# TensorE's order inside an expert step exchanged: the preceding expert's down products ahead of the next expert's up products

## The reference

```python
def step(state, xb_t):
    state = jnp.tanh(state @ A.T + xb_t)
    return (state, state)
out = jnp.einsum('bsn,dn->bsd', states, C) + D * x
y = out + x                                   # then layer norm, gamma, beta
x = _layernorm(x + y_normed)
...
scores = jax.nn.sigmoid(x @ router_weight.T)  # best group of four, best two of it
comb = (one_hot(topk_idx, E) * topk_w[..., None]).sum(1)
g = einsum('th,ehi->tei', x, w_gate); u = einsum('th,ehi->tei', x, w_up)
y = einsum('tei,eih->teh', silu(g) * u, w_down)
routed = einsum('teh,te->th', y, comb)
shared = silu(x @ sw_gate) * (x @ sw_up) @ sw_down
x = _layernorm(x + routed + shared)
```

## Time and profile before

| | us |
|---|---|
| median of 3 runs | 409.91 |
| lowest and highest | 409.0 and 410.25 |
| the profiled execution, whole | 411.52 |
| its span | 409.6 |
| scan, up to the first group | about 84 |
| one steady group (204 to 244) | 40.0 |
| TensorE busy in it | 38.75 |
| VectorE busy in it | 35.66 |

### The profile page before, as it was taken

The page is one execution under the profiler, slowest core; times in us unless marked ns, Lnnn a source line. Parts: engine busy times, 40 slices in busy tenths (PEclk is TensorE's granted clock), DMA queues, the critical chain, the costliest instruction groups (busy, mean ns, idle before and its releaser), DMA issues.

```text
span 409.6 us, 7468 instructions
## 1 busy us (share of the span) xinstructions
PE 377.2 (92%) x2563; PEld 248.1 (61%) x2563; DVE 324.3 (79%) x744; ACT 137.0 (33%) x276; POOL 160.1 (39%) x158
## 2 busy tenths in 40 slices
PE   6889996889899989998999899989998999999991
PEld 5889885445556555655665566556655666555560
DVE  2348998559786999699979997998799789974564
ACT  2455232132324232423242324243324333333330
POOL 1859018027433453344234513441354125423332
PEclk9999999689999999999999999999999999999997
DMA  7990000035005601560145016401840173009211
GB/s 204 305 317 4 0 2 0 2 94 115 2 0 104 106 2 51 100 109 1 53 113 96 1 53 129 78 0 53 133 71 0 53 150 57 36 20 165 40 53 51
DMA packets 15901, 29.95 MB, mean 73 GB/s; under 512 B 1720, under 2 KB 4288, under 8 KB 15872
## 3 DMA queue, kind: packets, MB, share of 16 engines
q1 hardware_dynamic: 15872, 29.58, 31.3%
HBM read 25.24 MB, written 4.33 MB: 72 GB/s over the span
## 4 chain that ended last, share of the span: by engine, by line
issue 28%; DVE 27%; PE 16%; POOL 14%; DMA 6%; SPq 5%; ACT 2%; POOLq 1%; DVEq 0%; ACTq 0%
PE bank L400 10%; POOL h L1008 10%; DVE st L722 4%; DVE wg L764 3%; PE bank L477 3%; POOL rstd L989 3%; DVE xT L879 3%; SPq L216 3%; DMA wu<-comb_dram 3%; DVE wu L755 2%; DMA xres<-in_L_attn_x_dram 2%; DVE xT L883 2%; DVE wu L747 1%; DVE wg L696 1%; ACT h L613 1%
## 5 line engine op out<-in xcount | busy, mean ns | idle before, releaser
L1008 POOL TENSOR_TENSOR h<-xT,h 128x512 f16<-128x512 f32 x72 | 86.1, 1195 | 192.7 <-ACT h L613 192.7
L400 PE MATMUL bank<-x2T,wg 128*128 128x512 f16 x432 | 107.4, 386 | 0.0
L477 PE MATMUL bank<-wd,h 128*128 128x256 f16 x864 | 106.1, 273 | 1.1 <-DVE wd L891 0.6
L400 PE MATMUL bank<-x2T,wu 128*128 128x512 f16 x432 | 106.5, 383 | 0.0
L477 PEld LDWEIGHTS bank<-wd,h 128*128 128x128 f16 x864 | 84.1, 98 | 25.6 <-issue 2.3
L613 ACT ACTIVATE h<-xT 128x512 f16<-128x512 f32 x72 | 45.4, 630 | 135.9 <-DVE xT L883 131.7
L400 PEld LDWEIGHTS bank<-x2T,wu 128*128 128x128 f16 x432 | 42.8, 99 | 52.7 <-issue 3.0
L879 DVE SCALAR_TENSOR_TENSOR xT<-bank,u_un,xT 128x512 f32<-128x512 f32 x64 | 47.5, 743 | 22.5 <-ACT xT L602 21.6
L400 PEld LDWEIGHTS bank<-x2T,wg 128*128 128x128 f16 x432 | 42.0, 99 | 37.1 <-issue 2.1
L602 ACT ACTIVATE xT<-bank,g_un 128x512 f32<-128x512 f32 x72 | 49.2, 683 | 35.8 <-PE bank L400 34.2
L313 PE MATMUL bank<-xT,BT 128*128 128x128 f32 x256 | 40.0, 279 | 0.0
(11 more groups left out here) (124 smaller groups left out, 370.0 us busy)
## 6 DMA issues: line engine op xcount, KB each, us to landing
comb_own<-comb_dram SPq DMA_DIRECT2D x32, 256.0 KB, 9.0
wu<-comb_dram SPq DMA_DIRECT2D x16, 256.0 KB, 4.1
wd<-comb_dram SPq DMA_DIRECT2D x16, 256.0 KB, 6.3
xres<-in_L_attn_x_dram SPq DMA_DIRECT2D x7, 512.0 KB, 6.6
out_dram<-xskip SPq DMA_DIRECT2D x7, 512.0 KB, 2.7
wd<-in_L_ffn_w_down_dram SPq DMA_DIRECT2D x1, 1024.0 KB, 6.9
xres<-in_L_attn_x_dram SPq DMA_DIRECT2D x2, 256.0 KB, 3.1
out_dram<-xskip SPq DMA_DIRECT2D x2, 256.0 KB, 2.0
```

What stands on the lines that cost most here:

```text
L400: last = pe.matmul(ps[:, :], w[:, pw, e, m // 3, :], x2T[:, par, px, m // 3, :], start=(m == 0), stop=(m == NUP // 2 - 1))
L477: return pe.matmul(ps_y[t // 2][:, (t % 2) * DM:(t % 2 + 1) * DM], h16[:, e % 3, ph, t * P:(t + 1) * P], wd16[:, pw, e, :], start=start, s ...
L1008: nc.gpsimd.tensor_tensor(h16[:, e % 3, 1, :], h[:, b, :], h16[:, e % 3, 0, :], ALU.subtract).then_inc(h_low, 1)
```

## The change

In `group` of TensorE the call of `down` for the preceding expert is moved ahead of the call of `up` for the next expert (and ahead of `turn_comb` in step 8). Nothing else is edited.

```diff
                 for e in range(E1):
                     b = (par + e) % 2
+                    if e:
+                        down(g, e - 1)
+                    elif not first:
+                        down(g - 1, E1 - 1)
                     if e < E1 - 1:
                         if e or not first:
                             up(g, e + 1, par, 1 - b)
                     elif not final:
                         up(g + 1, 0, 1 - par, 1 - b)
                         turn_comb(g + 1)
-                    if e:
-                        down(g, e - 1)
-                    elif not first:
-                        down(g - 1, E1 - 1)
                     if not final:
                         piece(e, g + 1, 1 - par, main)
```

## The result

| | before | after |
|---|---|---|
| median (lowest to highest), us | 410.08 (409.0 to 411.89) | 480.31 (478.84 to 481.75) |
| ratio | | 1.171, 95% interval 1.168 to 1.174 |
| span of the profiled execution | 409.6 | 476.8 |
| mean granted clock | 0.981 | 0.945 |

The account below looks back on a forecast made before the run. TensorE (92% busy) hardly waited before; in the new order VectorE's work sets each group's floor. Order 50 us plus clock 15 makes 65 on the 409.9 us median: 475 us, range 455 to 490 for 8 in 10.

Parts of the forecast that it names:

- the likeliest case: Whole kernel: new order and lower clock together give 465 to 485 us; chance 0.55.
- The floor by VectorE and the period: Steady group: VectorE's unshrinkable work gives a 44.9 us floor; with three late up products the period is 46.6 against 40.0.
- The order's total: Whole kernel without clock: six periods at 6.6 us, first group 5.8, last 4.7, sum 50.1 us.
- The wait ahead of D(0): TensorE ahead of expert 0's down products: waits 3.1 us for VectorE's closing sum, which comes after expert 1.
- The wait ahead of D(8): TensorE ahead of expert 8's down products: waits 2.6 to 3.0 us because VectorE's choice of experts can't shrink.
- The first group: First group: 1.9 us waiting for expert 0's low half, up products 1.31 later, expert 8's wait 2.6; together 5.8 us.
- The clock: TensorE at group boundaries: 9 of 14 waits drop the clock, 1.7 us each, 15 us; bounds 0 and 28.
- The clock stays up: Rival, whole kernel: clock stays at its upper level, 410 + 50 = 460 us; chance 0.20.
- The clock low at nearly every wait and slow to return: Rival, group boundaries: clock adds 28 us or more to the order's 50, giving 490 us; chance 0.12.
- Most of the wait absorbed: Rival: VectorE's idle time takes up late up products, only the 3.1 us closing-sum waits remain, some 432 us; chance 0.09.
- faster: Rival: earlier down products free halves and banks, transpose waits go, saving 10 us, 400 us; chance 0.02.
- no change: Rival: TensorE takes ready up products ahead of waiting down products, so the time stays 410 us; chance 0.02.

Follow-up runs that it names:

- the filled kernel: Changed kernel plus throwaway matmuls on TensorE, 10 ahead of expert 8's down products and 13 ahead of expert 0's, in every group but the first: 461.53 us, ratio 1.128.
- step 1 back: Changed kernel with step 1 alone in the old order, expert 2's up products ahead of expert 0's down products: 441.12 us, ratio 1.080.
- closing sum first: Changed kernel with VectorE's closing sum taken ahead of expert 1's gated product instead of behind its weighting: 444.54 us, ratio 1.086.
- the exchange there: Changed kernel with ScalarE, in step 8, making expert 8's high half ahead of the copy of the turned weights of choice: 478.03 us, ratio 1.167.
- the shorter choice: Changed kernel without VectorE's three tie-deciding operations: 477.57 us, ratio 1.168; with ScalarE's high half also ahead of its copy: 458.81 us, ratio 1.120.
- the last kernel: Kernel before, old order, with the transposes of steps 4 and 5 moved behind the next step's up products: 408.15 us, ratio 0.997.

## Why the prediction was right

The forecast was 475 us, the result 480.3, inside the range and inside the likeliest case's own.

- **The floor by VectorE and the period.** Summed 46.6 us, measured 46.94 with the clock held up. Right in its parts too. In the filled kernel it is 12.6 us from D(8) to the product of expert 2 (summed 12.5), 30.5 from there to product 8 (summed as 28.96 of work and 1.7 for three late U), and 3.79 from product 8 to the next D(8) (3.43). The three late U were summed as 0.5, 0.8 and 0.4 us and stand in the changed kernel at 0.43, 0.72 and 0.44. The last part is the one that was too short, by ScalarE's queue. The order's total was put at 50.1, it is 51.7.
- **The wait ahead of D(0)**, 3.1 us from U(1), SiLU, product, weighting and sum: measured 3.05 to 3.15, at the last boundary 3.7. Shown by two kernels that took it away (step 1 back, closing sum first).
- **The wait ahead of D(8)**, 2.6 to 3.0 from the choice of the experts: measured 2.4 to 2.8. The size was right, the reason was only one half. I followed VectorE's chain and left out ScalarE's queue; the exchange there and the shorter choice together show that both chains ended within 0.4 us of each other.
- **The first group**, 1.9 us ahead of D(0): measured 1.02 (D(0) at 85.80).
- **The clock**, 9 low stretches of 1.7 us, 15 us in all: eleven of 1.71, 18.8. The price was right, the count low by two. The clock makes 3.8 us of the 5.3 by which the forecast was short, the order 1.6. That the count came so near is in part luck: it was taken from three gaps, and waits of the same length cost none of seven and four of seven in two of the kernels above.
- **The rivals.** The clock stays up (460): rejected for the changed kernel, and the filled kernel is that case made real, at 461.5. The clock low at nearly every wait and slow to return (490): it fell at eleven of fourteen, but came back within 4 us each time, so the price was one U a fall. Most of the wait absorbed (432), faster, no change: rejected by the two waits.
- **The rule of the Trainium skill.** The Trainium skill (TensorE: Matmul & The Clock Gate, section on HAM oscillation) warns only of idle gaps longer than thirteen of these fourteen waits. Those thirteen, 2.4 to 3.2 us long, came with a fall ten times (the fourteenth, of 3.70 us, too), so the measurement decides against it.

What stays open: what makes a given wait cost the clock. With step 1 back, seven waits of 2.4 to 2.8 us at D(8) cost none; with the closing sum first, waits of the same length cost four.

## What to carry to other kernels

In a pipeline over several engines, the order on the engine that is hardly ever idle also sets the slack of all the others. Before you move a consumer up, compare the work left between producer and consumer with the whole chain between them. Here that was a D and a U, 3.9 us, against a chain of 4.4, and at the boundary one piece, 0.65 us, against 3.8 from the end of U(1) to the end of the closing sum. Look above all for waits other than the obvious one on the moved step: the dearest one here was a buffer's release (the closing sum), not the operand. And where two chains end at one instruction within a few tenths, an experiment that shortens only one will look as if that chain did not matter.

## What the runs showed of the hardware

- Waits of 2.4 to 3.7 us on TensorE amid dense work came with a fall of the granted clock from its upper level (2.4 GHz) to its lower (1.2) in eleven of fourteen cases in the changed kernel, at 1.7 us each, in four of seven with the closing sum first and in none of seven with step 1 back. The length of a wait alone doesn't decide it: a wait of 1.46 us had a fall behind it in the last kernel, one of 1.36 us had none. Matmuls whose results are thrown away, put into the wait, kept it at 1.00 and made the kernel 18.8 us faster.
- Shortening the waits paid twice. D(8) waiting 0.89 us instead of 2.5 saved 10.4 us of waiting and 8.5 us of low clock, as estimates from the two traces.
